# One message-passing kernel: every TensorE product split over four column tiles of 32

## The reference, cut to what matters

```
hi = einsum('bsh,hk->bsk', x, W1[:H]);  hj = einsum('bsh,hk->bsk', x, W1[H:])
h  = relu(hi[:, :, None, :] + hj[:, None, :, :] + b1)       # 128 x 128 x 128 a graph
y  = layernorm(einsum('bijk,kl->bijl', h, W2) + b2) * gamma + beta
x  = layernorm(x + einsum('bij,bijh->bih', adj, y))
# layer two: scores from two dot products, exp, times adj, row-normalized, times x, residual, layernorm
```

## Time and profile before

| | before |
|---|---|
| median of 3 runs | 2622.59 us |
| profiled execution, first to last instruction | 2621.4 us |
| PE busy | 2577.0 us (98%) |
| DVE busy | 2337.8 us (89%) |
| ACT busy | 2332.6 us (89%) |
| POOL busy | 1999.1 us (76%) |
| mean granted TensorE clock | 0.998 |

### The profile page before, as it was taken

The page is one execution under the profiler, slowest core; times in us unless marked ns, Lnnn a source line. Parts: engine busy times, 40 slices in busy tenths (PEclk is TensorE's granted clock), DMA queues, the critical chain, the costliest instruction groups (busy, mean ns, idle before and its releaser), DMA issues.

```text
span 2621.4 us, 77145 instructions
## 1 busy us (share of the span) xinstructions
PE 2577.0 (98%) x21263; PEld 2049.5 (78%) x21263; DVE 2337.8 (89%) x18135; ACT 2332.6 (89%) x3650; POOL 1999.1 (76%) x1163
## 2 busy tenths in 40 slices
PE   8999999999999999999999999999999999999997
PEld 7777777777777777777777777777777777777774
DVE  7889988989899889998898989988988999989897
ACT  7899899899998998989989889999899898998996
POOL 7777777777777777777777777777777777777773
PEclk9999999999999999999999999999999999999999
DMA  0000000000000000000000000000000000000000
GB/s 17 8 12 7 11 7 10 11 6 11 11 6 11 6 11 11 6 11 11 6 11 6 11 11 6 11 10 7 11 6 11 11 6 11 8 8 11 6 7 7
DMA packets 48051, 23.49 MB, mean 9 GB/s; under 512 B 6208, under 2 KB 47808, under 8 KB 47808
## 3 DMA queue, kind: packets, MB, share of 16 engines
q1 hardware_dynamic: 46512, 21.12, 2.9%
q10 hardware_dynamic: 1296, 0.20, 0.0%
HBM read 17.11 MB, written 4.19 MB: 8 GB/s over the span
## 4 chain that ended last, share of the span: by engine, by line
PE 58%; DVE 24%; issue 11%; ACT 6%; POOL 0%; ACTq 0%; DVEq 0%; DMA 0%
PE y_ps L529 42%; DVE squares L517 16%; PE agg_ps L573 12%; DVE q L517 3%; ACT y L263 3%; DVE x1e L488 2%; ACT h L281 1%; ACT L334 1%; PE prep_ps L529 1%; PE tail_ps L529 1%; DVE o_sb L455 1%; PE tail_ps L584 1%; PE att_ps L529 1%; DVE eT L509 0%; DVE si_cols L499 0%
## 5 line engine op out<-in xcount | busy, mean ns | idle before, releaser
L252 POOL TENSOR_TENSOR h<-bT,aT 128x1024 f32<-128x1024 f32 x1024 | 1951.1, 1919 | 584.3 <-PE y_ps L529 572.9
L529 PEld LDWEIGHTS y_ps<-w_pair,h 128*128 128x128 f32 x16384 | 1885.7, 192 | 313.0 <-DVE q L517 260.3
L529 PE MATMUL y_ps<-w_pair,h 128*128 128x128 f32 x16384 | 1991.3, 278 | 21.9 <-DVE q L517 9.3
L517 DVE CUSTOM_DVE_ANT_0 squares<-y_ps,y 128x128 bf16<-128x128 f32 x8192 | 1842.3, 282 | 185.0 <-ACT y L263 171.2
L263 ACT ACTIVATE y<-y_ps 128x508 f32<-128x508 f32 x2048 | 1162.4, 595 | 190.8 <-PE y_ps L529 173.9
L281 ACT ACTIVATE h<-h 128x1024 f32<-128x1024 f32 x1024 | 1085.3, 1060 | 10.2 <-POOL h L252 10.2
L517 DVE DVE_READ_ACCUMULATOR2_ANT q<- 128x1 f32 x8192 | 659.1, 80 | 0.0
L573 PE MATMUL agg_ps<-y,wz 128*32 128x512 f32 x4096 | 545.9, 606 | 1.7 <-DVE o_sb L455 1.7
L573 PEld LDWEIGHTS agg_ps<-y,wz 128*32 128x32 f32 x4096 | 81.1, 108 | 66.7 <-issue 3.1
L492 DVE CUSTOM_DVE_ANT_0 s_terms<-x1e,v1row 128x128 f32<-128x128 f32 x64 | 99.5, 1554 | 0.1
L334 ACT ACT_TABLE_LOAD x64 | 82.1, 1283 | 4.3 <-DVE sj L504 3.2
(11 more groups left out here) (90 smaller groups left out, 740.4 us busy)
## 6 DMA issues: line engine op xcount, KB each, us to landing
x_in<-in_x_dram SPq DMA_DIRECT2D x64, 64.0 KB, 1.8
adj_in<-in_adj_dram SPq DMA_DIRECT2D x64, 64.0 KB, 1.9
x_res<-in_x_dram SPq DMA_DIRECT2D x64, 64.0 KB, 1.8
adj_res<-in_adj_dram SPq DMA_DIRECT2D x64, 64.0 KB, 1.9
out_dram<-x_out SPq DMA_DIRECT2D x64, 64.0 KB, 1.6
w<-in_L_gnn_W_dram ACTq DMA_DIRECT2D x1, 64.0 KB, 2.4
w1a<-in_L_gnn_W_dram SPq DMA_DIRECT2D x1, 64.0 KB, 2.2
w1b<-in_L_gnn_W_dram SPq DMA_DIRECT2D x1, 64.0 KB, 2.3
```

Of the source, the lines that this page charges most:

```text
L252: nc.gpsimd.tensor_tensor(h[:, u % HRING].rearrange("k (r g) s -> k r g s", g=GROUPS), bT[:, p, :].unsqueeze(1).unsqueeze(1).broadcast_to( ...
L517: last = nc.vector.tensor_tensor_reduce(out=squares[:, k % YRING, n, :], in0=y_ps[k % YRING][:, n, :], in1=y[:, p, i, :], scale=1.0, scala ...
L529: return nc.tensor.matmul(dst, lhsT, rhs, start=start, stop=stop)
```

## The change

The helper `mm` now issues four products instead of one: column group g of the stationary operand goes to column tile g and writes the 32 partitions g of the destination. All products of the kernel go through it, the pair products too. The transpose instruction is gone: a transpose is now an ordinary product of the data, as the stationary operand, with the identity. The semaphore is raised by the last of the four. The weighted sums are as before. No other engine's code changes.

```diff
-            def mm(dst, lhsT, rhs, start=True, stop=True):
-                return nc.tensor.matmul(dst, lhsT, rhs, start=start, stop=stop)
+            def mm(dst, lhsT, rhs):
+                for g in range(GROUPS):
+                    cols = slice(g * GROUP, (g + 1) * GROUP)
+                    last = nc.tensor.matmul(dst[cols], lhsT[:, cols], rhs, start=True, stop=True, tile_position=(0, g * GROUP))
+                return last
...
-                nc.tensor.transpose(prep_ps[:, 0, :], x_in[:, p, :], ident[:]).then_inc(xT_ps_s, 1)
+                mm(prep_ps[:, 0, :], x_in[:, p, :], ident[:]).then_inc(xT_ps_s, 1)
...
-                        nc.tensor.transpose(tail_ps[:, 0, :], o_sb[:], ident[:]).then_inc(oT_ps_s, 1)
+                        mm(tail_ps[:, 0, :], o_sb[:], ident[:]).then_inc(oT_ps_s, 1)
...
-                        nc.tensor.transpose(tail_ps[:, 3, :], si_cols[:], ident[:]).then_inc(score_ps_s, 1)
+                        mm(tail_ps[:, 3, :], si_cols[:], ident[:]).then_inc(score_ps_s, 1)
```

More of the change, by code:

```diff
@@ L535, in prep_transposes @@
                     pe.wait_ge(ab_sb_s, b)
-                nc.tensor.transpose(prep_ps[:, 0, :], x_in[:, p, :], ident[:]).then_inc(xT_ps_s, 1)
+                mm(prep_ps[:, 0, :], x_in[:, p, :], ident[:]).then_inc(xT_ps_s, 1)
                 pe.wait_ge(adj_loaded[p], loads)
-                nc.tensor.transpose(prep_ps[:, 1, :], adj_in[:, p, :], ident[:]).then_inc(adjT_ps_s, 1)
+                mm(prep_ps[:, 1, :], adj_in[:, p, :], ident[:]).then_inc(adjT_ps_s, 1)
             def prep_products(b):
@@ L552, in _ @@
             mm(att_ps[:, 0:1], centre[:], b2col[:]).then_inc(s_setup_pe, 1)
-            nc.tensor.transpose(tail_ps[:, 0, :], w2[:], ident[:]).then_inc(s_setup_pe, 1)
+            mm(tail_ps[:, 0, :], w2[:], ident[:]).then_inc(s_setup_pe, 1)
             mm(tail_ps[:, 1, :], a1rep[:], ww[:]).then_inc(s_setup_pe, 1)
```

## The result

The changed kernel takes 2653.58 us, the median of four runs (2651.43 to 2656.35); the kernel before takes 2622.68 beside it (2622.38 to 2622.78). The ratio is 1.0119, with a 95% interval of 1.0104 to 1.0133. The forecast was 2523, with a range of 2450 to 2595: wrong in its sign.

A forecast was written before the change was run, and what follows sets the result against it. PE was taken as the bound, in a close race with DVE. The terms gave 2621.4 - 104 - 25 + 14 + 15 = 2521, with 1.2 us for the median of the runs 2523 us; range 2450 to 2595.

The forecast's parts named there:

- What bounds the kernel: PE is the bound, busy 40.3 of a 40.40 us slot, in a close race with DVE.
- DVE has 3.7 us a slot free: DVE works 36.7 us of a 40.40 us slot; used as evidence against the gain turning into waits.
- Parts 1 to 3: PE: switch drains go (104 us), pair products' rounds take 109 ns (25 us), transposes in two rounds cost 14 us.
- Part 4: PE's larger loop body leaves the engine: pause at the loop's start, 0.5 us a pass, +15 us, ends 0 and 70.
- The sum: Whole kernel: all terms give 2521 us, 38.9 us a slot, against DVE's 37.6 in the loop.
- meetings such as unit 13: PE's first pair load right after DVE's `q`; such existing meetings were left 1.5 us a slot.
- drains, cadence and code: The forecast's spread: PE's switch drains 60 to 170 us, pair rounds' cadence 0 to 42, PE's code pauses 0 to 70.
- The gain turns into waits: Rival: PE gets faster but waits for `q` and `si_cols` everywhere, 2617 to 2628 us; chance 0.05.
- Small tiles stream badly: Rival: pair products' rounds take 135 ns instead of 111.6, total 2833 us, or near 4700 with slow instructions; chance 0.08.
- code comes too slowly: Rival: PE pauses at every q8 code packet, a slot grows by 13 us, the total to 3450 us; chance 0.05.
- DVE's wait for `y` falling: Sign expected in the profile after: DVE's wait for `y` smaller than 171.2 us.
- PE's slot shrinking by 3 us with the run by under 1%: Sign of refutation: PE's slot shrinks by 3 us while the whole time shrinks by less than 1%.

The follow-up runs named there:

- e1: Kernel before with its hardware loop written out as plain code, nothing else changed: 2616.59 us, ratio 0.9977.
- e6: Kernel before with each of POOL's additions split into two of half the size: 2609.67 us, ratio 0.9949.
- e3: Changed kernel with each of POOL's additions split into two halves, loop kept: 2579.94 us, ratio 0.9834.
- e9: Changed kernel, loop written out, POOL's additions whole, `eT` one pair of squares earlier and `v` three pairs later: 2512.75 us, ratio 0.9581.
- e5: Changed kernel with the loop written out and POOL's additions in halves: 2497.17 us, ratio 0.9519.
- e2: Changed kernel with its hardware loop written out, nothing else changed: 2633.37 us, ratio 1.0040.
- e4: Changed kernel with only DVE's `eT` moved one pair of squares earlier (about 0.42 us): 2616.85 us, ratio 0.9977.
- e11: Changed kernel with POOL's additions in halves and four slots a loop pass instead of two: 2551.82 us, ratio 0.9735.
- e8: Kernel before with four slots a loop pass instead of two, no product newly tiled: 2638.77 us, ratio 1.0061.

## Why the prediction was wrong

**What bounds the kernel: right before, wrong after.** PE was the bound. But the step from "DVE has 3.7 us a slot free" to a DVE that keeps up took DVE's durations as fixed. After the change the chain that ended last lies on PE for 39% of the span instead of 58%:

```profile
PE 39%; ACT 25%; DVE 20%; issue 14%; ACTq 1%; DMA 0%; DVEq 0%; POOL 0%
```

**Parts 1 to 3: right.** The drains are gone, the rounds take 109 ns, the starts within one are 6 to 7 ns apart, and the transposes are two rounds. Their sum was 104 + 25 - 14 = 115 us. With both causes away the kernel is 2622.72 - 2497.17 = 126 us below before; before itself would gain some 6 and 13 us by the same edits (e1 and e6, if they add up, which was not run), so the change alone is worth about 106. The TensorE side was right within a tenth.

**Part 4: the pause is real, its price was wrong.** I took 0.5 us a pass since "DVE makes its own pause at the same place". It doesn't do so at the same time. PE's pause ends at 1235.62; DVE, behind PE, reaches its own branch later and has `v` at 1238.57 after 1.82 us:

```profile
1238.57 0.29 DVE L413 TENSOR_SCALAR v<-q,bnorm 128x128 f32<-128x128 f32 x1 [1.82 <-issue]
...
1238.75 1.91 POOL L252 TENSOR_TENSOR h<-bT,aT 128x1024 f32<-128x1024 f32 x1 [4.68 <-PE y_ps L531]
```

The pauses come one behind the other, and POOL, at the end of the line, stood 4.68 us. The measured price is 83 us with the meetings cured, above even my end of 70, and 20 with them. (Writing out takes DVE's branch away too, which in e1 was worth 6 us, and some 15 of the 83 are the lower clock behind the pauses, which the term left out.) The mechanism was right and the term mis-sized: 15 taken. The body before has 1328 loads and matmuls, not 1344; nothing hangs on that.

**The sum: the step that failed.** "The sum (38.9 us a slot) leaves 1.5 us a slot for meetings such as unit 13, which exist already; I keep it." (38.9 less the 37.6 of the sentence before is 1.3.) The term for new or longer meetings was nothing. It held all other engines' durations constant under a shift of their times. The earlier trace rows give DVE 36.7 us a slot; the two slots after have more.

```profile
1197.00:1239.40 42.40, 38.40 (x1136) 31.81 (x1132) 38.80 (x289) 35.97 (x58) 30.99 (x19) 0.97 0.05 13
1239.40:1279.60 40.20, 37.97 (x1160) 31.74 (x1156) 36.64 (x278) 35.92 (x57) 30.88 (x19) 0.99 0.05 12
...
sum 82.60, PE 76.38 PEld 63.55 DVE 75.44 ACT 71.89 POOL 61.87; mean PE 38.19 PEld 31.77 DVE 37.72 ACT 35.94 POOL 30.93
```

37.7 us a slot here, and by the page's sums 108/64 = 1.7 us a slot more than before in the whole run, with the growth at the two places that PE or the whole pipeline waits for: `eT`, before PE's first product of a slot, and `v`, before DVE's squares. The evidence lay in the trace before: `eT` had a mean of 490 ns where `x1p` of the same size had 286, and `s_terms` had 1554 and 1044 ns. Here a step much longer than its equals was held by a neighbour, and what held it could hold it longer. What this cost the run is read from the cures: 74 us by halves alone (e3), 121 by places and 136 by halves once the loop is written out (e9 and e5 against e2), where the sum had nothing. The stated range was narrow besides: its own ends for drains, cadence and code, added up, reach from 2425 to 2647 and not from 2450 to 2595.

**The rivals.** "The gain turns into waits" (2617 to 2628, chance 0.05) was nearest in kind, though for `q` and `si_cols`, for which PE's waits rose only from 9.3 to 40.9 us and from 2.9 to 27.4, while `eT` took 67.6. "Small tiles stream badly" and "code comes too slowly" are refuted: 109 ns a round, and 1.5 us in all in which PE waited for nothing but its instructions before pair products, while q8 brought 633 packets. None of the rivals named a longer step on an untouched engine, which was the cause. My signs listed DVE's wait for `y` falling (171.2 to 113.7 us: it did) and PE's slot shrinking by 3 us with the run by under 1% as what would refute me. What came is of that kind: PE's busy time shrank by 141/64 = 2.2 us a slot, and the run grew.

**What stays open.** What each meeting costs the run can't be read from its length: `eT`'s 91 us and `v`'s 59 are DVE's busy time, e4 and e9 are the time of the run. Why some of e11's pauses last 3.4 to 3.7 us and the others 2.1 to 2.5, and why the clock fell behind some of the pauses in e3, e4 and after the change and not behind others, is not shown. That before and after, freed of both causes, differ by 106 us rests on adding e1 and e6.

## What to carry to other kernels

Before a change that speeds up one engine of a balanced pipeline, list the steps of the other engines whose mean is far above that of steps of the same size: they may be held by a neighbour, and the shift will move them to a better or worse place in its instruction; here moving one step by 0.4 us changed the run by 37 us. When several causes may cover each other, remove them together as well as one by one (20 and 74 us, and 156 together). Where one product becomes four, count the loop body's instructions before asking what the products cost.

## What the runs showed of the hardware

- The DVE steps `eT`, `s_terms` and `x_beta` (two inputs in SBUF) end 0.15 us, and `v` and `x1e` (`TENSOR_SCALAR`, one tensor input in SBUF) 0.08 us, behind the end of the POOL addition that runs when they start: `v` takes 0.29 us when it meets none and up to 1.8 when it meets one. Not every step with its operands in SBUF is held: the reciprocal `rstd` (948 and 942 ns) and the statistics `st` of `x1p` (290 and 291) stay as they are, like `x1p` with its PSUM operand. A step can also be held by the next one: in e5 `s_terms` of L505 starts 0.08 us before the end of a half (1234.68 and 1234.76), takes 1.23 us and ends 0.15 behind the half after it.
- A taken branch of PE into code that is not on the engine holds it for 2.85 us on the timeline (1.56 with the body of 2656 loads and matmuls in e8). Much the same amount of code in sequence, some 16 KB for every 4 us, costs next to nothing: in e5, PE's idle time before pair products with nothing to wait for but its instructions is 2.3 us in all, in e2 7.3.
- After the pause at 1232.77 to 1235.62 the granted clock fell to its lower level, 1.2 GHz, for a while:

```profile
1232.80:1236.80 4.00, 1.18 (x44) 1.00 0.03 6
1236.80:1240.20 3.40, 3.40 (x75) 0.50 0.03 7
1240.20:1244.00 3.80, 3.80 (x124) 1.00 0.00 0
```

(stretch, us, PE busy and count, granted clock). That is why the 32 rounds at 1235.86 take 5.35 us instead of 3.68, 1.7 more. In this run it happened behind 5 of the 28 pauses, the mean clock being 0.995 against 0.998, so it is a small part of the loss: the run with a clock of 0.998 still took 2651.43 us. In e4 (19 of 28) and e11 (13 of 13) it is a larger one. In the kernel before, which has no such pause, the clock was at the lower level only in the last tail, from 2598 us on; it was not at the upper level quite throughout.
